# A four-layer transformer kernel: null keys' weights kept in token layout, their scores moved to GpSimd, and later blocks prepared last on VectorE

## The reference

```python
k = concatenate([nk, k]); v = concatenate([nv, v])       # nk, nv: 2 null keys/values per head
q = l2norm(q) * q_scale;  k = l2norm(k) * k_scale
sim = einsum('bhid,bhjd->bhij', q, k) * 8
sim = sim + dist * slopes                                # a linear distance bias, per head
attn = softmax(where(causal_mask, -max, sim))
x = x + einsum('bhij,bhjd->bhid', attn, v) @ w_out
```

## Time and profile before

| what | value |
|---|---|
| median of the runs | 2654.86 us |
| the profiled execution's own time | 2653.18 us |
| its span in the trace | 2651.5 us |
| TensorE busy (matmuls) over the span | 2391.5 us (90%) |
| VectorE busy | 1726.2 us (65%) |
| ScalarE busy | 1484.6 us (56%) |
| GpSimd busy | 1602.2 us (60%) |
| mean granted clock of TensorE | 0.964 of full speed |

### The profile page before, as it was taken

One profiled execution on the slowest core, in us unless ns is written; L12 is line 12 of the kernel. 1 busy time (PEld: TensorE's weight loads), 2 busy tenths in 40 slices (PEclk: granted clock), 3 DMA queues, 4 the chain that ended last, 5 costly groups with the idle time before them and its releaser, 6 DMA issues. The chain is left out here.

```text
span 2651.5 us, 62747 instructions
## 1 busy us (share of the span) xinstructions
PE 2391.5 (90%) x24121; PEld 1872.9 (71%) x24121; DVE 1726.2 (65%) x4520; ACT 1484.6 (56%) x3071; POOL 1602.2 (60%) x2517
## 2 busy tenths in 40 slices
PE   3999999999997788898999899999999867689896
PEld 3888888888885555565777788777777657455555
DVE  4677777777774667774544467777777622576766
ACT  3666666666663457774444466666666423366674
POOL 4677778787775644443433267777777711666554
PEclk9999999999998969999999999999999979799998
DMA  3692000000000010000000000000000045000000
GB/s 113 205 334 73 2 2 2 2 2 2 2 2 1 9 45 2 2 2 1 22 1 1 3 2 6 6 6 4 6 6 6 6 147 162 14 10 8 4 2 32
DMA packets 23257, 83.12 MB, mean 31 GB/s; under 512 B 4113, under 2 KB 11026, under 8 KB 21938
## 3 DMA queue, kind: packets, MB, share of 16 engines
q1 hardware_dynamic: 19810, 71.90, 8.4%
q0 software_dynamic: 3152, 7.21, 0.8%
HBM read 71.89 MB, written 46.79 MB: 45 GB/s over the span
## 5 line engine op out<-in xcount | busy, mean ns | idle before, releaser
L855 POOL TENSOR_TENSOR XR<-XR,T 128x256 f32<-128x256 f32 x512 | 375.5, 733 | 159.0 <-DVE T L736 128.8
L613 ACT ACTIVATE P<-ps 128x384 f32<-128x384 f32 (+1 forms) x512 | 250.8, 542 | 180.4 <-PE ps L2479 179.0
L2479 PE MATMUL ps<-P,V 128*64 128x256 f32 (+3 forms) x4096 | 333.6, 347 | 5.8 <-DVE O L1352 4.6
L1336 DVE TENSOR_REDUCE bm<-ps 128x3 f32<-128x384 f32 x512 | 260.4, 550 | 105.4 <-PE ps L2479 104.8
L2479 PEld LDWEIGHTS ps<-P,V 128*64 128x64 f32 (+1 forms) x4096 | 185.7, 123 | 123.6 <-issue 30.0
L1263 ACT ACTIVATE P<-ps 128x768 f32<-128x768 f32 x256 | 207.8, 812 | 98.0 <-PE ps L2479 95.8
L747 DVE TENSOR_REDUCE sm<-ps 128x2 f32<-128x512 f32 (+1 forms) x256 | 130.8, 553 | 181.0 <-PE ps L2479 179.9
L1432 POOL TENSOR_SCALAR_AFFINE_SELECT P<-P 128x512 f32<-128x512 f32 x256 | 162.7, 635 | 127.7 <-ACT P L1263 125.4
L868 POOL TENSOR_TENSOR PS<-P 128x256 f32<-128x256 f32 x256 | 181.4, 732 | 70.9 <-ACT P L613 70.4
L2479 PE MATMUL ps<-mk,identb 128*128 128x256 bf16 (+1 forms) x1024 | 203.6, 294 | 14.8 <-DVE bm L1336 12.7
L876 POOL TENSOR_TENSOR ss<-ss,nhalf 128x16 f32<-128x16 f32 x64 | 187.8, 2934 | 5.3
(11 more groups left out here) (323 smaller groups left out, 7147.3 us busy)
## 6 DMA issues: line engine op xcount, KB each, us to landing
rows_i<-in_zero SPq DMA_DIRECT2D x16, 1208.0 KB, 31.6
rows_o<-in_zero SPq DMA_DIRECT2D x16, 1208.0 KB, 80.0
w<-in_m_w SPq DMA_DIRECT2D x23, 578.0 KB, 4.0
zt<-rows_i SPq DMA_DIRECT2D x23, 128.0 KB, 3.1
rows_o<-yo POOLq DMA_DIRECT2D x23, 128.0 KB, 3.8
stg<-in_t_w SPq DMA_DIRECT2D x11, 256.0 KB, 2.7
XR<-in_x SPq DMA_DIRECT2D x4, 512.0 KB, 8.3
out<-XR SPq DMA_DIRECT2D x8, 256.0 KB, 2.0
```

What stands on the lines that cost most here:

```text
L613: e.activation(self.P[at % 6][:, :], K.ps.ap("st", s, g, h)[:, 0:self.w], ACT.Exp, bias=0.0, scale=1.0 if kind == 0 else 0.125).then_inc(K ...
L855: p = po.e.tensor_tensor(x, x, self.T[g % 2][:, par, pr], ALU.add)
L1336: e.tensor_reduce(bm[:, h, :], K.ps.ap("mx", s, g, h)[:, 0:384].rearrange("p (a c) -> p a c", c=128), X, ALU.max, negate=True).then_inc(K. ...
L2479: return self.te.matmul(o, l, r, start=start, stop=True, skip_group_check=True)
```

## The change

Four things change, all in stage 0.

1. The null keys' weights stay in token layout. `pn` is now 128 tokens by 64 (two token tiles, 16 heads, two null keys) and is filled by one multiplication per unit, exponential times reciprocal sum, on GpSimd at k = 22, ahead of `pool_sum`. Once a block, a new item "null" transposes it (k = 0), multiplies it with `nvw` (k = 1), and VectorE adds the product to `XR` (k = 2). `nvw` is null values times output weights, made once by eight matmuls. The three matmuls per unit at `pv`, the two transposes of `pn` at `mT` and ScalarE's copy of them are gone, as are GpSimd's three copies, and VectorE's preparation of `nvs` and `nvo`.
2. The softmax sum gets the null part in token layout: GpSimd adds the two exponentials of each head (k = 12), VectorE adds that to the sums ahead of the reciprocal.
3. The null scores' multiplication and addition move from VectorE at k = 8 to GpSimd at k = 3, behind the scaling of `raw`, each as one instruction over 16 elements a partition. VectorE keeps the maximum.
4. VectorE walks an order of its own, in which `prep` comes last in its tick.

The next stage waits for VectorE's addition of a block (`done`) in place of GpSimd's last sum. The stage's first staging transfers change places: the five of `KB` come first, and one of `nvs` behind them replaces three.

```diff
+            if kind == 0:
+                items.append((16 * b + first + 12 + unit, 2, "null", (b,), 3))
...
+        self.dve_order = ticks(items, self.dve_rank)
...
-        return self.summed, 4 * b + 4
+        return self.K.ps.read("nul", self.s, b) if self.kind == 0 else (self.summed, 4 * b + 4)
...
+        if name == "null":
+            return 3 if k == 0 else 2
...
+    def dve_rank(self, name, k):
+        return 6 if self.kind == 0 and name == "prep" else self.rank(name, k)
...
+                if self.kind == 0 and a == (0, 0) and k == 8:
+                    self.pe_nvw(pe)
...
+    def pe_nvw(self, pe):
...
+        for j in range(8):
+            p = pe.e.matmul(ps[0:64, 0:128], K.stg[n % 2][:, 64 * j:64 * j + 64], K.wO[:, 128 * j:128 * j + 128],
+                            start=j == 0, stop=j == 7)
...
+    def pe_null(self, pe, b, k):
...
+        if k == 0:
+            ps = K.ps.take(pe, self.G, "pnT", s, b)
+            pe.wait_ge(self.shared, 4 * b + 4)
+            K.tr(ps[0:64, 0:128], self.pn[b % 2][:, :]).then_inc(K.ps.full_of("pnT", s, b), 1)
+        if k == 1:
+            ps = K.ps.take(pe, self.G, "nul", s, b)
...
+            K.acc(ps[:, 0:256], self.pnT[b % 2][:, :], self.nvw[:, :], start=True).then_inc(K.ps.full_of("nul", s, b), 1)
...
-            if kind == 0:
-                pe.wait_ge(self.pnull, g + 1)
-                for i in range(2):
-                    p = K.tr(ps[0:96, 256 + 128 * i:384 + 128 * i], fv(self.pn[g % 2][:, i, :]))
...
-            for pr in range(2):
-                c = 256 * u + 128 * pr
-                K.acc(pv[:, 256 * pr:256 * pr + 256], self.nvs[:, 0, c:c + 128], self.pnT[g % 2][:, :], start=pr == 0)
-            K.acc(sm[:, 0:256], self.nvo[:, 4 * u:4 * u + 4, :].rearrange("p h c -> p (h c)"), self.pnT[g % 2][:, :],
-                  start=True)
...
-            if kind == 0:
-                i = e.activation(self.pnT[g % 2][:, :], ps[0:96, 256:512], ACT.Copy)
...
+            elif name == "null":
+                if k == 2:
...
+                    dv.wait_ge(self.summed, 4 * b + 4)
+                    dv.wait_ge(*K.ps.filled("nul", self.s, b))
+                    e.tensor_tensor(xs, K.ps.ap("nul", self.s, b)[:, 0:256], xs, ALU.add).then_inc(
+                        K.ps.out_of("nul", self.s, b), 1)
...
+            if kind == 0:
+                dv.after(dv.step(e.tensor_tensor(rs[:, :], sums, self.sm[g % 4][:, 48:56], ALU.add)))
+            e.reciprocal(rs[:, :], rs[:, :] if kind == 0 else sums).then_inc(K.ps.out_of("sT", s, g), 1)
...
-        for t in range(2):
-            d = dv.step(e.tensor_tensor(sn[:, t], snr[:, t], rq[:, t].to_broadcast([128, 2, 2, 2]), ALU.mult))
-        dv.after(d)
-        for t in range(2):
-            d = dv.step(e.tensor_tensor(sn[:, t], sn[:, t], nb, ALU.add))
-        dv.after(d)
...
+    def pool_null(self, po, g):
...
+        po.after(po.step(e.tensor_tensor(sn, snr, rq, ALU.mult)))
+        e.tensor_tensor(sn, sn, nb, ALU.add).then_inc(self.scored, 1)
...
+            self.pool_null(po, g)
         if k == self.tk["mx"] + 3:
...
-            d = po.step(e.tensor_copy(pn[:, :, 0:8], s6))
-            e.tensor_copy(pn[:, :, 64:72], s6)
-            po.after(d)
-            e.tensor_tensor(pn[:, :, 32:40], s6, fv(pn[:, :, 0:8]), ALU.subtract).then_inc(self.pnull, 1)
+            ex = sm[:, 32:48].rearrange("p (a n) -> p a n", n=2)
+            e.tensor_tensor(sm[:, 48:56], ex[:, :, 0], ex[:, :, 1], ALU.add).then_inc(self.pnull, 1)
+        if k == self.tk["out"]:
...
+            po.wait_ge(*K.ps.read("sT", s, g))
+            e.tensor_tensor(
+                self.pn[b % 2][:, :].rearrange("p (t h n) -> p t h n", t=2, n=2)[:, :, 4 * u:4 * u + 4, :], ex,
+                self.rs[g % 2][:, :].rearrange("p (t h) -> p t h", t=2).unsqueeze(3).to_broadcast([128, 2, 4, 2]),
+                ALU.mult).then_inc(self.shared, 1)
```

More of the change, by code:

```diff
@@ L64, in __init__ @@
         self.lies = [{i} for i in range(8)] + [{2 * i, 2 * i + 1} for i in range(4)]
-        self.full, self.out = ([sem(f"{n}{i}") for i in range(12)] for n in ("full", "out"))
+        self.full, self.out = ({i: sem(f"{n}{i}") for i in (0, 1, 2, 3, 4, 5, 6, 7, 10)} for n in ("full", "out"))
         self.n, self.turn, self.table = [0] * 12, {}, {}
@@ L182, in __init__ @@
             self.sn = [sb(f"sn{s}_{i}", [128, 64], F32) for i in range(2)]
[L183 to L186, removed]
+            self.pn = [sb(f"pn{s}_{i}", [128, 64], F32) for i in range(2)]
+            self.pnT = [sb(f"pnT{s}_{i}", [64, 128], F32) for i in range(2)]
+            self.nvw = sb(f"nvw{s}", [64, 256], F32)
             self.on = sb(f"on{s}", [128, 128], F32R)
@@ L477, in pe_pv @@
                 for h in range(4):
-                    p = K.acc(sm[32 * h:32 * h + 32, q:q + w], self.one[:, 0:32], P[h][:, c:c + w])
+                    p = K.acc(sm[32 * h:32 * h + 32, q:q + w], self.one[:, 0:32], P[h][:, c:c + w], start=kt == 0)
             p.then_inc(K.ps.full_of("sm", s, g), 1)
@@ L513, in act @@
                 a[0].act(ac, a[1], k)
+            elif name == "null":
+                if k == 0:
+                    b = a[0]
+                    if b >= 2:
+                        ac.wait_ge(*self.K.ps.filled("nul", self.s, b - 2))
+                    ac.wait_ge(*self.K.ps.filled("pnT", self.s, b))
+                    ac.e.activation(self.pnT[b % 2][:, :], self.K.ps.ap("pnT", self.s, b)[0:64, 0:128], ACT.Copy).then_inc(
+                        self.K.ps.out_of("pnT", self.s, b), 1)
             elif name == "unit":
@@ L533, in act_kb, with act_nvw @@
             e.activation(o, i, ACT.Copy).then_inc(self.kb_in, 1)
+    def act_nvw(self, ac):
+        K = self.K
+        ac.wait_ge(self.nv_zero, 1)
+        ac.wait_ge(*K.ps.filled("nvw"))
+        for t in range(2):
+            r = slice(32 * t, 32 * t + 32)
+            i = ac.e.activation(self.nvw[r, 128 * t:128 * t + 128], K.ps.ap("nvw")[r, 0:128], ACT.Copy)
+            i.then_inc(*((K.ps.out_of("nvw"), 1) if t else (self.nvs_in, 1)))
     def act_prep(self, ac, b, k):
@@ L591, in act_unit @@
             if g >= 4:
[L592 removed]
+                ac.wait_ge(self.shared, g - 3)
             ac.wait_ge(self.nul, g + 1)
@@ L638, in dve @@
                 K.ps.out_of("beff"), 1)
-        for name, a, k in self.order:
+        for name, a, k in self.dve_order:
             if name == "prep":
@@ L814, in pool @@
         if self.kind == 0:
-            for pn in self.pn:
-                e.memset(fv(pn[:, :, :]), 0.0).then_inc(K.pn_in, 1)
+            e.memset(self.nvw[:, :], 0.0).then_inc(self.nv_zero, 1)
         for name, a, k in self.pool_order:
@@ L899, in sp @@
         if self.kind == 0:
-            for n, (a, b) in enumerate(((0, 512), (512, 1024), (1024, 1040))):
-                n += self.nvs_at
-                K.sp_stage(sp, n, K.stg[n % 2][0:96, 0:b - a], K.t["nvs"][:, a:b])
             for c in range(5):
```

105 lines of the change are left out of this document (52 added, 53 removed).

## The result

The changed kernel takes 2691.03 us (median of 4 runs, 2687.05 to 2701.82) against 2652.87 us (4 runs): a ratio of 1.0146, 95% interval [1.0119, 1.0174]. Its profiled execution took 2687.7 us, with a span of 2686.0. Forecast were 2686 us and a range of 2640 to 2712.

The account below looks back on a forecast made before the run. Stage 0 was taken to run at the pace of TensorE's program. 2653.2 - 46.5 + 9.6 + 2 + 36.4 + 20.2 + 1 = 2675.9 us, plus 10.5 for the clock, gave 2686 us, range 2640 to 2712.

Parts of the forecast that it names:

- The boundary wait: At block boundaries TensorE waits 2.6 us for GpSimd's scaling of raw, behind late VectorE statistics; 14 blocks, +36.4 us.
- The bank wait: TensorE's masks wait 1.35 us for the null item's PSUM bank, until VectorE's addition reads it; 15 blocks, +20.2 us.
- The saving on TensorE: Removed pn transposes (0.22 us) and nvs, nvo matmuls (0.53) save 0.75 us a unit; 62 units, -46.5 us.
- a deviation to the other side: Named as making the forecast wrong altogether: a TensorE saving per unit much above 0.75 us.
- The additions: TensorE's added transpose and full-precision matmul cost 0.6 us a block, 9.6 in all; making nvw once adds 2.
- The clock: TensorE's clock falls behind half of the 14 longer waits, losing 1.5 us each: +10.5 us, bounds 0 and 49.
- The sum: All terms added to the profiled 2653.2 us gave 2675.9 us, and 2686 us with the clock's 10.5.
- VectorE's and GpSimd's other work: VectorE's lost operations are worth nothing; GpSimd's net +0.5 us a unit hides in its idle time; stage end and filling +1.
- rival F: GpSimd becomes the bound if its two score operations cost over 1.4 us: 2739 us, chance 0.03.
- A: Both TensorE waits come and the clock falls little or half the time: 2668 to 2700 us, chance 0.58; the forecast.
- C: TensorE's saving decides and neither wait comes: 2619 us, chance 0.10.
- two places with little slack: TensorE's transposes of raw, with 0.8 us to spare after a block's second prep, and the PSUM ring, turning in under two ticks.

Follow-up runs that it names:

- Experiments 4: The kernel before with only VectorE's own order added (prep last in its tick): 2691.90 us, ratio 1.0148 to the kernel before.
- 10: The changed kernel with GpSimd's second rstd of a block put behind its sum: 2664.76 us, ratio 1.0041 to the kernel before.
- experiment 2: The changed kernel with VectorE's addition of the null product put first in its tick: 2676.51 us, ratio 1.0085 to the kernel before.
- experiment 7: The kernel before without the null keys' five TensorE operations a unit and ScalarE's copy, output incomplete: 2631.13 us, ratio 0.9928 to the kernel before.
- experiment 8: As experiments 5, with the null scores' multiplication and addition back on VectorE at k = 8: 2641.05 us, ratio 0.9965 to the kernel before.
- experiments 3: The changed kernel with VectorE's common order restored and the null addition first in its tick: 2648.83 us, ratio 0.9982 to the kernel before.
- experiments 5: The changed kernel with the null addition first and GpSimd's second rstd of a block behind its sum: 2643.63 us, ratio 0.9972 to the kernel before.
- Experiment 9: As experiments 5, with VectorE's z and second statistics of a block one tick later, behind KL: 2643.11 us, ratio 0.9961 to the kernel before.
- experiment 6: As experiments 3, with GpSimd's two score operations moved from k = 3 to k = 4: 2637.18 us, ratio 0.9948 to the kernel before.

## Why the prediction was right

**The boundary wait.** Right in place and cause, and somewhat too large in size. GpSimd's `rstd` begins 5.04 us after the maxima, worked out were 5.07; the sum at 6.94, worked out 7.1. The wait is 2.2 to 2.3 us start to start, forecast 2.6. The forecast took TensorE to come 0.75 us earlier; in this unit it came only 0.38 earlier (11.82 to 11.44). The table agrees: 1.64 across the wait and the 0.56 that the unit saves make 2.2. Experiments 4 (the order alone makes it) and 10 (GpSimd's order alone takes it away) show the cause.

**The bank wait.** 1.39 us against 1.35, and experiment 2 takes it away.

**The saving on TensorE** is the term that was mis-sized. I priced the three matmuls from 516.15 to 516.68 at 0.53 us. Without them `P,V` begins 0.53 us after the second transposes of `raw` where `nvs` began after 0.35, so 0.18 of the 0.53 was a pause ahead of `P,V` that stays. The rhythm says it directly: 11.72 to 11.16, 0.56 a unit, and experiment 7 by stage 0 alone 0.61. Over 62 units that is 35 to 38 us in place of 46.5. I had named a deviation to the other side as what could go wrong.

**The additions.** Per block the transpose of `pn` puts `P,V` 0.63 us behind the second transposes of `raw` where 0.53 is usual, 0.10 more. With the product the masks begin 0.84 us behind the last matmul ahead of it (491.95 to 492.79), where 0.12 is usual. Together 0.8 in place of 0.6.

**The clock.** It fell 8 times; I had taken half of 14. Each fall made a unit 1.1 to 1.6 us longer (in most 15.81 for 14.64), forecast 1.5: 10 us, forecast 10.5. In the changed kernel all falls past the filling came at waits for `raw`; none at a bank wait of 1.4 us. The half was a guess between two rows, and that it came out was luck.

**The sum.** By the four lines of the rhythm table a block changes by -0.56 - 0.38 + 1.64 + 1.66 = +2.36 us (forecast +1.55). Of the 0.8 between, the smaller saving of four units is 0.8, the additions 0.2 and the masks that wait for `KL` 0.2, and the shorter wait for `raw` takes 0.4 back. 14 times 2.36 is 33 us, and 10 for the clock: 43. Ahead of the first wait the changed kernel is 3.6 us early (maxima at 110.97 for 114.59), which leaves 39.4; the mark moved by 39.1. The forecast had 33 for all of it. That 2686 came so near the profiled 2687.7 is in part luck: the later stages, which the change doesn't touch, happened to be 4.6 us shorter in that execution.

**VectorE's and GpSimd's other work.** I had priced it at nothing, and experiment 8 agrees for the scores. GpSimd's two score operations take 0.22 us each for 16 elements a partition, so rival F never came near. The Trainium skill (GPSIMD Engine Reference, 4.1 Engine selection) would have had GpSimd slower for this, at about half VectorE's speed; no such factor shows for operations this small. But the prediction's 0.427 us for VectorE's 8 elements is a mean of unlike times. For the multiplication, with a mean of 0.403, the source view before says:

```profile
L800 DVE TENSOR_TENSOR sm<-sn,ss x84: 152/160/705, 254.0 to 748.4; 128x8 f32<-128x8 f32 x84
```

The median is 0.16 us. All 84 ran beside GpSimd's additions to `XR`. In experiment 8, 20 of them ran beside its operations on one element a partition, and those took 0.16 us each.

**The rivals.** A came. For C more than two edits would have been needed: experiments 3, 5 and 9 show that with both waits removed a third comes up, `KL`, which I had not seen. The prediction put no price on the `prep` ahead of `KL` and named only two places with little slack. There is a third: before, `KL` ended at 495.59 and TensorE's masks came at 495.74, 0.15 us of slack, less than the change's own saving. Experiment 9, with 0.7 us of waits left a block, ends stage 0 16 us earlier than before, where C's 2619 needed 34; the smaller saving and the larger additions account for most of that. VectorE's order, as changed, trades a wait of 1.0 us for one of 2.2 and a clock that falls.

What stays open: why the rest of the kernel differs by up to 14 us between profiled executions, what makes the clock fall at some waits for `raw` and not at others of the same length, and whether experiment 6 or 9 is the faster: their steady blocks are equally long and their intervals overlap.

## What to carry to other kernels

When one engine is full, ask of every reordering on another engine whose queue holds a wait for the moved work, and what is queued behind that wait: here statistics made 2 us later held up a sum, the sum the norms, and these the full engine, at 2.2 us a block. Take the time of a removed instruction from start to start, and then look at what the next instruction would have waited for anyway. After a saving on the full engine recheck each margin that is smaller than the saving: here `KL` had 0.15 us, and in experiment 7 the cut alone brought its wait up. And ask what an engine that is freed will run beside: GpSimd's additions, let through early, made VectorE's `z` more than twice as long. A mean duration can hide such a thing; look at the least and the most as well.

## What the runs showed of the hardware

The clock of TensorE, at 2.4 GHz in the steady part of stage 0 before, went to 1.2 GHz for some 3.4 us at waits of under 2 us in the records (1.87 to 1.89), in a stream that was dense otherwise, and from 269 us on at every second of them, blocks being 51 us apart. The Trainium skill (TensorE: Matmul & The Clock Gate, Part 1) ties a fall to a whole idle window; by that rule alone these waits should rather have been harmless. In the changed kernel no fall came at a bank wait of 1.4 us.

VectorE's `z` on 128x128 took 0.33 to 0.35 us while GpSimd was idle or worked on one element a partition, and 0.59 to 0.90 us in each of the 62 cases beside GpSimd's 256-wide additions (experiments 5, 9 and 10, 250 to 750 us). No run here shows why.
